# Latent attention of a 16-block hybrid network: maxima from bf16 parts, spread over all steps, with the product between them

## What is computed

```
c_q = h_t @ W_DQ + b_DQ                        # 32 wide
c_kv = h_t @ W_DKV + b_DKV                     # 32 wide
q = [c_q @ W_UQ + b_UQ, c_q @ W_QR + b_QR]     # per head, 128 + 32 wide
k = [c_kv @ W_UK + b_UK, h_t @ W_KR + b_KR]
attn = softmax(q @ k.T / sqrt(160))
o = attn @ (c_kv @ W_UV + b_UV)
return o @ W_O + b_O
```

## Time and profile before

| what | us |
|---|---|
| median of 3 runs | 4385.51 |
| the profiled execution, its own time | 4400.56 |
| its span in the profile | 4398.8 |
| PE busy | 3628.2 (82%) |
| DVE busy | 3012.3 (68%) |
| ACT busy | 2482.7 (56%) |
| POOL busy | 1168.0 (27%) |
| maxima of the latent block on DVE, 256 | 302.3 |
| its exponentials on ACT, 256 | 257.8 |
| its additions on POOL, 140 + 14 | 328.4 + 32.9 |

### The profile page before, as it was taken

How to read it: one execution, slowest core, us unless ns; L and a number is a source line. 1 busy time by engine, 2 the same in 40 slices (tenths; PEclk the granted TensorE clock), 3 DMA queues, 4 the chain that set the end, 5 groups by cost and what they waited for, 6 DMA issues and landing times. The chain is left out here.

```text
span 4398.8 us, 86825 instructions
## 1 busy us (share of the span) xinstructions
PE 3628.2 (82%) x33381; PEld 1655.7 (38%) x33381; DVE 3012.3 (68%) x4370; ACT 2482.7 (56%) x4824; POOL 1168.0 (27%) x1181
## 2 busy tenths in 40 slices
PE   5769998754888888687999997778995779999957
PEld 4523333633222222342222223355654612222237
DVE  6567774557565665658999994435994489999933
ACT  3436665463144444433888886434543548888844
POOL 2610000524465664000000000035883500000016
PEclk7879999876799999896999998878996879999979
DMA  3221110210000000002000000140001120000012
GB/s 122 70 78 38 40 42 15 83 32 9 2 4 5 7 4 5 18 0 71 27 25 31 31 21 3 27 116 14 1 1 63 57 76 25 31 31 23 20 54 73
DMA packets 82885, 153.20 MB, mean 35 GB/s; under 512 B 22940, under 2 KB 49196, under 8 KB 81580
## 3 DMA queue, kind: packets, MB, share of 16 engines
q1 hardware_dynamic: 56856, 105.74, 7.6%
q0 software_dynamic: 12704, 22.97, 1.8%
q10 hardware_dynamic: 12916, 18.93, 1.3%
HBM read 103.76 MB, written 31.20 MB: 31 GB/s over the span
## 5 line engine op out<-in xcount | busy, mean ns | idle before, releaser
L1516 DVE TENSOR_REDUCE 55_heads_mx<-55_heads_mps 128x1 f32<-128x1024 f32 x512 | 602.8, 1220 | 49.1 <-PE 55_heads_mps L1366 46.7
L1516 DVE TENSOR_REDUCE 32_heads_mx<-32_heads_mps 128x1 f32<-128x1024 f32 x512 | 602.7, 1220 | 47.5 <-PE 32_heads_mps L1366 45.1
L1486 ACT ACTIVATE 55_heads_p<-55_heads_sps 128x512 f32<-128x512 f32 x1024 | 553.7, 596 | 86.2 <-PE 55_heads_sps L1392 83.0
L1486 ACT ACTIVATE 32_heads_p<-32_heads_sps 128x512 f32<-128x512 f32 x1024 | 553.7, 596 | 85.9 <-PE 32_heads_sps L1392 82.5
L2581 ACT ACTIVATE 21_latent_heads_p<-21_latent_heads_ring 128x1024 f32<-128x1024 f32 x256 | 257.8, 1024 | 350.9 <-PE 21_latent_heads_ring L2486 348.5
L1516 DVE TENSOR_REDUCE 7_heads_mx<-7_heads_mps 128x1 f32<-128x1024 f32 (+7 forms) x384 | 333.8, 909 | 147.7 <-PE 7_heads_mps L1374 100.9
L1486 ACT ACTIVATE 7_heads_p<-7_heads_sps 128x512 f32<-128x512 f32 (+3 forms) x640 | 308.1, 533 | 156.2 <-PE 7_heads_sps L1395 116.5
L2610 DVE TENSOR_REDUCE 21_latent_heads_mx<-21_latent_heads_ring 128x1 f32<-128x1024 f32 x256 | 302.3, 1220 | 130.0 <-PE 21_latent_heads_ring L2465 130.0
L2395 POOL TENSOR_TENSOR 21_latent_heads_psum<-21_latent_heads_psum,21_latent_heads_p 128x1024 f32<-128x1024 f32 x140 | 328.4, 2349 | 85.8 <-ACT 21_latent_heads_p L2581 81.0
L1392 PE MATMUL 55_heads_sps<-51_head_rows_qs,51_head_rows_ks 123*32 123x512 bf16 x4096 | 314.3, 383 | 8.3 <-ACT 55_heads_p L1486 5.0
L1392 PE MATMUL 32_heads_sps<-30_head_rows_qs,30_head_rows_ks 123*32 123x512 bf16 x4096 | 314.1, 383 | 8.4 <-ACT 32_heads_p L1486 5.0
(11 more groups left out here) (1217 smaller groups left out, 6778.8 us busy)
## 6 DMA issues: line engine op xcount, KB each, us to landing
3_routed_experts<-in_L0f_experts SPq DMA_DIRECT2D x8, 514.0 KB
9_routed_experts<-in_L0f_experts SPq DMA_DIRECT2D x8, 514.0 KB, 6.5
50_routed_experts<-in_L3f_experts SPq DMA_DIRECT2D x8, 514.0 KB
57_routed_experts<-in_L3f_experts SPq DMA_DIRECT2D x8, 514.0 KB
38_hale_masks_qs<-scratch_q_parts SPq DMA_DIRECT2D x11, 288.0 KB
38_hale_masks_ks<-scratch_k_parts SPq DMA_DIRECT2D x33, 96.0 KB
yT<-scratch_results SPq DMA_DIRECT2D x12, 256.0 KB, 6.3
y<-scratch_results ACTq DMA_DIRECT2D x12, 256.0 KB, 6.6
```

What stands on the lines that cost most here:

```text
L1486: act.activation(pslot[x % PS][:, 0:CW - off], sps[e % SB][:, 0:CW - off], ACT.Exp, scale=SCALE / 2).then_inc(ex_done, 1)
L1516: dve.tensor_reduce(mx[h % 2][:, i, half:half + 1], mps[x % 2][:, 0:w], AX.X, ALU.max).then_inc(mx_taken, 1)
```

## The change

**Maxima.** A unit is now two bf16 matmuls of 99 rows and nothing else. The rows are three products of parts and the tilt: `rough_q` holds the queries rounded to bf16 in rows 0 to 63 and what the rounding left in rows 64 to 95; `rough_k` holds the head keys rounded in rows 0 to 31 and 64 to 95 and the remainder in rows 32 to 63; three more rows are ones against the three tilt parts. ACT rounds each half of the head keys after copying it (`take_keys`, a second activation), DVE subtracts (`rest_of_keys`). The maxima differ from the fp32 ones by what the left-out product of the two remainders holds; they only shift the exponent.

**Scores.** The tilt is no longer in the scores' bf16 matmul but is the exponential's bias, one column per key tile (`tilt_bias`). The bf16 matmul subtracts the maxima only, with `minus` (all -1) as weights and three rows per row group in `q_side`, which is now 512 wide: row group c holds the maxima of query chunk c. So scores of step p use row groups 2(p % 2) and 2(p % 2) + 1. `queries` holds chunk c of the queries in row group c.

**Order.** One maxima unit goes with each step, six ahead (`AHEAD`), from step 0 on; on PE a pair of steps is now scores, scores, maxima unit, product of the pair before, maxima unit. Keys are made two heads ahead, at steps 17 and 21, into three buffers `kh`. The turning is at step 29, the denominators at step 9 (5 in the last head). DVE runs three steps behind with its additions (`LAG`), ACT copies the denominators, and the reciprocal comes in four pieces at steps 11 to 14.

**Additions.** `BY_DVE` is 26 to 31: POOL has 24 additions a head and DVE 4. In the last head POOL has the even steps below 24 (11 additions).

**DMAs.** The maxima go to `q_side` in twelve DMAs of 1 KB a head (3 parts x 4 chunks) and not four of 12 KB. The tilt of a head takes one DMA and not four.

```diff
-    SUMS = 6
-    FIRST, LAST = 6, 24
-    TURNED = 28
-    MAKE = (FIRST - 1, FIRST + 1)
-    BY_DVE = tuple(range(24, S))
+    AHEAD = 6
+    SUMS = 9
+    MAKE = (17, 21)
+    TURNED = 29
+    LAG = 3
+    INVERT = (11, 12, 13, 14)
+    BY_DVE = tuple(range(26, S))
...
+        def with_dve(h, p):
+            return p in BY_DVE if h < LASTH else p % 2 == 1 or p >= 24
...
+        def maxima_at(h, p):
+
+            v = h * U + p + AHEAD
+            return [(1 + v // U, v % U)] if v < U * LASTH else []
...
                 for h in range(MLA_H):
                     sp.wait_ge(m_copied, h + 1)
-                    for top in range(0, P, DC):
-                        sp.dma_start(q_side[h % 2][top + 3:top + 6, :], mT[h % 2][0:PARTS, :]).then_inc(m_in[h % 2], 16)
+                    for c in range(NC):
+                        for a in range(3):
+                            at = a * NT + TPC * c
+                            sp.dma_start(q_side[h % 2][DC * c + a:DC * c + a + 1, :], mT[h % 2][at:at + TPC, :]).then_inc(m_in[h % 2], 16)
+                    if h + 2 < MLA_H:
+                        sp.wait_ge(sc_ready, 2 * S * h + 1)
+                        load_tilt(h + 2)
...
                     for x in range(2):
-                        r = rows(number, x)
-                        pe.matmul(bank(number, x), cq[r, tile(i)], kh[h % 2][r, chunk(2 * pair + x)], start=True, stop=False,
-                                  tile_position=(r.start, 0))
...
+                        ins = pe.matmul(bank(("max", h, u), x), rough_q[0:K_ROWS, tile(i)], rough_k[h % 2][0:K_ROWS, chunk(2 * pair + x)],
+                                        start=True, stop=True)
+                    ins.then_inc(mx_ready, 1)
...
+                        pe.matmul(bank(("score", h, p), x), kh[h % 3][r, tile(p // 2)], queries[r, :], start=True, stop=False,
+                                  tile_position=(DC * c, 0))
...
+                        pe.matmul(bank(("score", h, p), x), minus[r, :], q_side[h % 2][r, :], start=False, stop=True,
+                                  tile_position=(DC * c, 0)).then_inc(sc_ready, 1)
...
+                for u in range(4):
+                    max_pair(0, u)
+                for pair in range(2):
+                    make_keys(1, pair)
+                for u in range(4, U):
+                    max_pair(0, u)
+                for u in range(AHEAD // 2):
+                    max_pair(1, u)
                 pe.wait_ge(tilt_copied, 1)
                 turn_max(0)
+                for u in range(AHEAD // 2, AHEAD):
+                    max_pair(1, u)
+                pe.wait_ge(tilt_scaled, 1)
                 for h in range(MLA_H):
                     for p in range(S):
-                        scores(p, h)
-                        if p == 0 and h:
-                            product(NT - 1, h - 1)
-                        if p == SUMS and h:
-                            denominators(h - 1)
...
+                        scores(h, p)
+                        if p % 2:
+                            for unit in maxima_at(h, p - 1):
+                                max_pair(*unit)
+                            if p > 1:
+                                product(h, p // 2 - 1)
+                            elif h:
+                                product(h - 1, NT - 1)
+                            for unit in maxima_at(h, p):
+                                max_pair(*unit)
+                        if h + 2 < MLA_H and p in MAKE:
+                            make_keys(h + 2, MAKE.index(p))
+                        if h and p == sums_at(h):
                             denominators(h - 1)
+                        if h + 1 < MLA_H and p == TURNED:
                             turn_max(h + 1)
...
+                    act.activation(rough_k[h % 2][0:TRIPLE, at], kh[h % 3][0:TRIPLE, at], ACT.Identity).then_inc(k_rounded, 1)
...
+                        act.activation(slot(p, h)[:], pair_of(("score", h, p))[:], ACT.Exp, scale=MLA_SCALE,
+                                       bias=tilt_bias[:, h, p // 2:p // 2 + 1]).then_inc(ex_done, 1)
...
+                def rest_of_keys(h, pair):
+                    dve.wait_ge(k_rounded, 2 * h + pair + 1)
+                    low = rough_k[h % 2][DC:KC, half_of(pair)]
+                    dve.tensor_tensor(low, kh[h % 3][DC:KC, half_of(pair)], low, ALU.subtract).then_inc(k_rest, 1)
```

324 lines of the change are left out of this document (165 added, 159 removed).

## The result

The kernel after the change takes 4423.12 us (median of 5 runs, 4413.57 to 4434.69), the one before 4385.51 (5 runs beside them, 4383.36 to 4391.16): ratio **1.0085**, 95% interval 1.0063 to 1.0107. Forecast were 4297 us, 4245 to 4350. The miss is 126 us. In the profiled execution (span 4428.2 us, 29.4 more) the next norm starts at 1843.51 us and not at 1809.85; so the loss is in the latent heads. Five heads from copy to copy of the maxima, 1234.09 to 1686.79 us, take 90.5 us each, where they took 83.1 before and 71.4 were forecast.

The account below looks back on a forecast made before the run. PE's work bounded the kernel, POOL's additions just under it; after the change POOL would. Head 0 -14.1, six heads -70.2, last head -5.5, tail +1.2 sum to -88.6 us: 4385.5 to 4297 us, range 4245 to 4350.

Parts of the forecast that it names:

- What bounds, and the rows: Latent heads before the change: PE's work limits, POOL's 22 additions (51.7 us a head) just under; a head takes 83.1 us.
- POOL becomes the bound: Middle of a head: POOL's 24 additions, 56.4 us, set the pace and hide DVE's, ACT's and PE's extra work.
- PE's pair of steps: PE within a head: two score passes 1.36, two maxima passes 0.43 each, product 1.00, together 3.2 us.
- exp(29) waits for the addition of step 23: End of a head: this exponential starts 4.7 us before POOL's last addition ends, the maxima copy 3.6 us before.
- ACT's exponentials waiting for POOL where they now wait for PE: Sign of a right forecast: within a head, ACT runs ahead of POOL, at most some five exponentials.
- The change of head: Between heads: twelve DMA issues 8.8 us, PE idle some 8 us, restart at reduced clock to first addition 8.1 us.
- Rival A: Change of head: twelve smaller DMAs issue in the time of four; head 63.5 us, kernel 4232 us; chance 0.18.
- Rivals B and C: PE's clock: B, returns late after each restart, 4339 us, chance 0.21; C, stays low within heads, 4590 us, chance 0.07.
- Rival **D: Latent heads: additions were already the bound, a head stays near 83 us, kernel 4385 us; chance 0.04.
- Last head: Last latent head: POOL takes even steps, so 57.5 us where it took 63.0, a gain of 5.5 us.
- Tail: Last exponential to next norm: denominators over two sums +1.0, reciprocal in four +0.2, together +1.2 us.
- Bias operand: ACT's exponentials: the bias adds 0.1 us each, hidden while POOL is the bound, 0.1 to 0.3 at each start.

Follow-up runs that it names:

- Experiment 2: Kernel after the change, with PSUM operands for DVE's multiply, key remainders (taken one step behind) and split of the maxima: 4319.3 us, 0.9849.
- experiments 10 and 11: Kernel of experiment 4 with POOL's additions a head changed from 24 to 22 (4308.1 us, 0.9819) and to 26 (4278.7 us, 0.9761).
- experiment 4: Kernel of Experiment 2 with the maxima's rows sent in three DMAs a head and not twelve: 4276.4 us, 0.9756.
- experiment 12: Kernel of experiment 4 with all additions of the last head on DVE, none on POOL: 4271.1 us, 0.9742.

## Why the prediction was wrong

**What bounds, and the rows:** the rows are right as read. What was missed is that 0.69 us for the multiply and 0.17 for a cast are prices beside a POOL that pauses.

**The step that failed** is in "POOL becomes the bound": POOL's train hides "on DVE two key remainders of at most 1.22 us each (they are narrower than a maximum)", and "DVE and ACT are far from full". DVE's busy share was the wrong measure. The multiply, the remainders and the split had no term of their own for what POOL's new train does to them. By the forecast's own terms, for the head from 1324.65 to 1415.50 us: copy to POOL's first addition 17.8 (18.6 forecast); first addition to the end of the last 66.0 (56.4), with 5.5, 2.4 and 0.7 us of idle time behind the multiply and two additions of over 3 us, beside which DVE got in; from there to the next copy 7.1 later (3.6 earlier), with the exponentials behind POOL and not ahead of it, and the split held for 4 us. Experiment 2, with the holds taken out, gives 4319 us, inside the range forecast, and prices them (with the moved remainder) at 104 of the 126 us.

The Trainium skill, "SBUF — State Buffer", section "Who interferes with whom", says that a DVE instruction with two SBUF inputs contends with a GpSimd instruction that reads SBUF, that copies and casts can, and a tensor_reduce never does. The traces agree (11.70, 10.57 and 0.15 us), and it would have been the rival to name. Of DVE's two-port modes it also says that the engine which issues first has the shared ports for its whole instruction; here a hold lasted through the addition under way and four or five more of POOL's, so the measurement goes beyond it.

**PE's pair of steps:** 3.2 forecast. The undisturbed one is 3.58 us (exponentials at 1349.27 and 1352.86). The pieces hold (two score passes 1.36, product 1.0); a maxima pass takes 0.53 to the next start and not 0.43, and the rest is likely the hand-off over ACT to the ring's next bank behind the second score pass, which no run takes out.

**A second step failed, and the holds hide it:** "exp(29) waits for the addition of step 23", which puts the copy 3.6 us before the end of POOL's last addition. In experiment 2 the holds are gone and the additions run back to back (56.3 us, 56.4 forecast), but the copy comes 2.3 us after that end, 5.9 us later than forecast; the way from the copy to the first addition is 1.8 shorter (16.8 and 18.6). That is 4 us more in each of the five middle heads, about the size of the rest of the miss, 22 us. The exponentials did not wait for POOL: over the whole block of experiment 2 ACT is idle before them for 224.0 us until PE and for 8.8 until POOL. The sign that was named, "ACT's exponentials waiting for POOL where they now wait for PE", is not there even without the holds, and experiments 10 and 11 agree. So that 4319 us lies in the range is in part luck; that the longer pair on PE alone keeps ACT from getting ahead is likely but not shown.

**The change of head:** right in the sum. Twelve issues 7.46 us (8.8 forecast), PE idle 4.73 before the scores (some 8 forecast), then half clock, restart to first addition 8.9 (8.1). Rival A (twelve issues in the time of four, 0.24 us each) is refuted at 0.6 us each.

**Rivals B and C, the clock:** 0.83 to 0.91 in stretches of 80 us from 1180 to 1820 us, so lower than before's 0.98, but it followed the stops and vanished with them (0.93 in three heads of experiment 2, 0.99 in experiment 4). C was the only case that had the kernel slower, and named PE's clock as the place; the kernel did get slower, by another mechanism. Rival **D** (nothing changes) named the right doubt, that "something else keeps it idle", but not the thing.

**Last head:** 57.5 us forecast, 58.3 measured (1770.23 to 1828.56 us, the end of the last exponential); but that it fits is luck in part: the shared additions were to save time and cost it (experiment 12). **Tail:** from there to the next norm 14.9 us, forecast 11.2 (10.0 before): DVE is still at its additions when the last exponential ends. **Bias operand:** 0.09 us, right.

## What to carry to other kernels

When a change takes the gaps out of one engine's work, price the instructions of the others that read the same memory anew: their old durations were measured in the old gaps. Look for the short instruction with all operands in SBUF on DVE that stands beside a train of POOL instructions, and give it a PSUM operand, another place, or a gap in the train. Here products and subtractions of two inputs, copies, casts and a scale-and-add were held at least once; reciprocals and maxima never. An engine's low busy share says nothing on this. Count DMA issues by number and not by bytes where something waits for the last of them.
